# A vision tower's last chunk: its delta solve and output moved from a stage of their own into the end stage

## The chip, the cores and the metric

The kernel runs on one core of a Trainium2 chip. A core has a matrix engine (PE, with its weight loads, PEld, shown apart), a vector engine (DVE), a scalar engine (ACT), a general engine (POOL) and a sync engine (SP), which here only issues DMAs. Each engine takes its own instructions in order, and they wait for one another by semaphores. The time is the device time of one execution in microseconds (us); lower is better. Before the change it was 1849.73 us, the median of 3 runs (1849.12 to 1850.84).

## The reference, cut to what matters

64 images become sequences of 38 tokens (36 patches and 2 class tokens) of width 256. Two layers follow. The first is softmax attention and a mixture of experts. The second, which is where the change lies, is a delta-rule layer with a gated, normalised output, and a feed-forward network with ternary weights:

```python
def step(S, inp):                       # per head, over the 38 steps of an image
    qt, kt, vt, at, gkt = inp
    Sp = S * jnp.exp(gkt)[..., None]
    u = jnp.einsum('bhk,bhkv->bhv', at, Sp) + vt
    S = Sp + jnp.einsum('bhk,bhv->bhkv', kt, u)
    o = jnp.einsum('bhk,bhkv->bhv', qt, S)
    return (S, o)
...
gate = jax.nn.sigmoid(x @ Wg1 @ Wg2)
out = out * gate
mu = jnp.mean(out, axis=-1, keepdims=True)
var = jnp.mean(jnp.square(out - mu), axis=-1, keepdims=True)
out = (out - mu) * jax.lax.rsqrt(var + 1e-05) * norm_w
return out @ Wo
...
scale = jnp.maximum(jnp.mean(jnp.abs(w)), 1e-08)      # ternary weights of the FFN
w_t = jnp.clip(jnp.round(w / scale), -1.0, 1.0)
```

## The kernel before, in words

All activations stay in the core's memory: the residual `RES` by 19 tiles of 128 tokens, and the normalised input transposed, as a high and a low part (`XH`, `XL`), since products are made from split numbers. The program is a row of stages. A stage (`stage`) is a block in which every engine has its own list of instructions; at its end all engines meet at a barrier and the semaphores are cleared, so nothing of one stage runs beside another.

The delta rule is solved by chunks of 8 images, `CHUNKS` = 8. The recurrence of a chunk becomes a triangular system for u, and the work on it is a pipeline over the stages `delta_stage(..., c, nxt, z, y)`, called for k = 0 to 10: stage k projects chunk k (`nxt`), scores chunk k-1 (`c`), inverts the triangular blocks of chunk k-2 (`z`) and solves and outputs chunk k-3 (`y`). So the last stage, k = 10, has only `y` = 7.

The solve has 64 lanes (4 pairs of images by 16 heads), in two halves of 32, `j` (or `i`) = 0 and 1. For each half PE runs `first_half`, 64 small matmuls of the inverse with the values; ACT copies the result back (`first_back`, into `RX`); `remainder`, 64 matmuls, multiplies it with the off-diagonal block; DVE scales this and adds the values (`with_values`, two operations); `second_half`, 64 matmuls, uses the inverse again; ACT copies (`solution`); and `output`, 32 matmuls, gives the outputs of even and odd heads in PSUM banks. ACT and DVE then put the two together (`odd_out`, `whole_out`, into `OW`) and write high and low parts into `XH` and `XL` (`high_out`, `low_out`). One such fp32 matmul is two matmul instructions with two weight loads in the trace: the stage k = 10 has 448 in the program and 896 in the trace.

Then comes the end stage, `output_tail`. SP loads the FFN's weights (`ffn_w`, 1 MB twice, and the biases). PE makes for each tile t the gate (`gate`, one matmul) and the delta output in token rows (`token_rows`, four matmuls against the identity). ACT takes the sigmoid into `SG`, DVE multiplies it with the rows (`gated`, into `Y`) and takes statistics. The first 9 tiles (`LEAD`) and all 19 gates are done ahead of a loop. Still ahead of it DVE sums the weights' magnitudes (L1616), PE adds them over the partitions (L1481), DVE makes the scales (L1620 to L1624) and the inverse deviations of the first 9 tiles. The loop's turn j then normalises tile j (ACT L1502), transposes it (PE L1446, ACT L1507, DVE L1574), multiplies tile j-1 by the output weights (PE L1459), adds it to the residual with statistics (DVE), and normalises and transposes the sum of tile j-3 (L1517, L1470, L1522, L1600), with DVE's L1593 and L1595 for its scale and shift; it also makes the token rows and products of tile j+9. POOL meanwhile turns the weights to ternary, 16 slices of three operations (L1652 to L1657), as soon as the scales are there. The last stage, `ternary_ffn`, is the FFN.

Buffers are taken from one stack of memory. Those of the delta stages (`delta_buffers`) are given back before the FFN's weights get their place, in the same memory.

Of the kernel before, what the change touches and what calls it, by code (L numbers as in the profile page):

```python
# [18 lines left out]
F32 = mybir.dt.float32  # L19
# [295 lines left out]
def build_tower(nc, ins, out):  # L315
    with ExitStack() as whole:
        numbers = count()

        def sb(ctx, name, shape, dt=F32):
            name = f"{name}_{next(numbers)}"  # L320
            return ctx.enter_context(nc.sbuf_tensor(name, shape, dt))
# [964 lines left out]
def last_layer(nc, sb, psum, bank, ins, RES, BN, MV, STD, XN, XH, XL, xh_c, xl_c, ident, identb, hmask, out):  # L1286
# [9 lines left out]
    with ExitStack() as ctx:  # L1296
# [54 lines left out]

        with ExitStack() as inner:
            b = delta_buffers(sb, inner, XN)
# [11 lines left out]
        with ExitStack() as own:  # L1365
# [8 lines left out]
            Y = sb(own, "gated_out", [P, TILES, D])  # L1374
            SG = sb(own, "gate", [P, TILES, D])
# [3 lines left out]
                        w1, w2, b1, b2, up, down, ones, S, flat, tern, Y, SG, shift, eps)  # L1379
# [8 lines left out]
def output_tail(nc, bank, ins, RES, BN, MV, STD, XN, XH, XL, ident, identr, G1, wg2s, woh, wol,  # L1388
                w1, w2, b1, b2, up, down, ones, S, flat, tern, Y, SG, shift, eps):
# [4 lines left out]

    with stage(nc, "f_loaded", "eps_set", "ones_set", "abs_sum", "f_sum", "scale", "cut", "is_up", "is_down", "tern",
               "g_tile", "gate_ready", "o_tile", "y_ready", "bn_1", "mv_1", "std_1", "inv_1", "shift_1", "normed_1",
               "turned_1", "hi_1", "lo_1", "product", "summed", "bn_2", "mv_2", "std_2", "inv_2", "shift_2", "normed_2",
               "turned_2", "hi_2", "lo_2") as (
# [3 lines left out]
            turned_2, hi_2, lo_2):  # L1402
# [7 lines left out]
        def two_halves(tile):  # L1410
            return tile.rearrange("p (m t) -> p m t", m=HALVES)

# [7 lines left out]
        def _(pe):  # L1420
            def gate(t):
# [4 lines left out]
                nc.tensor.matmul(bank[2 + t % 2][:, 0:D], G1[:, cols(t)], wg2s[:, :],  # L1426
                                 start=True, stop=True).then_inc(g_ready, 1)

            def token_rows(t):
                if t >= TILES:  # L1430
                    return
                if t >= 2:
                    pe.wait_ge(y_ready, t - 1)
                for m in range(HALVES):
                    nc.tensor.matmul(bank[t % 2][:, m * P:(m + 1) * P], XH[:, m, cols(t)], identr[:, :],
                                     start=True, stop=False)
                    mm = nc.tensor.matmul(bank[t % 2][:, m * P:(m + 1) * P], XL[:, m, cols(t)], identr[:, :],
# [3 lines left out]
            def turn_gated(t):  # L1441
                pe.wait_ge(normed_1, t + 1)
                if t >= 2:
# [6 lines left out]
            def project(t):  # L1450
                pe.wait_ge(lo_1, t + 1)
                if t == 1:
                    pe.wait_ge(scaled, 1)
                if t >= 2:
# [8 lines left out]
            def turn_sum(t):  # L1463
                pe.wait_ge(normed_2, t + 1)
                if t < 2:
                    pe.wait_ge(gate_ready, TILES)
# [7 lines left out]
            for t in range(LEAD):  # L1474
                gate(2 * t)
                gate(2 * t + 1)
                token_rows(t)
            gate(2 * LEAD)
            pe.wait_ge(abs_sum, 2)
            pe.wait_ge(ones_set, 1)  # L1480
# [1057 lines left out]
```

## Time and profile before

| What | us |
|---|---|
| Median of 3 runs | 1849.73 (1849.12 to 1850.84) |
| The profiled execution's own time | 1850.91 |
| Its span in the trace | 1848.9 |
| PE busy | 1649.3 (89%) |
| DVE busy | 1103.9 (60%) |
| ACT busy | 689.7 (37%) |
| POOL busy | 332.6 (18%) |
| Stage k = 10, first to last instruction | 1664.68 to about 1690.5 |
| Gates and first token rows | 1691.17 to 1704 |
| Loop of the end stage | 1710.24 to 1767.8 |
| FFN | 1767.8 to 1848.9 |

Times within the trace are counted from the span's start. Busy PE counts overlapping matmuls, so it is not PE at its peak. "Idle before" in brackets is how long the engine stood before a row, and the name behind the arrow who released it; "issue" means that it waited for nothing that the profile shows, PEq for its own sequencer.

### The profile page before, as it was taken

How to read it: one execution, taken by the hardware profiler on the slowest of the kernel's cores; microseconds unless marked ns; L12 is line 12 of the kernel's file. 1: busy time of each engine (PE TensorE's matmuls, PEld its weight loads, DVE VectorE, ACT ScalarE, POOL GpSimd, SP SyncE). 2: the span in 40 equal slices, each digit the busy share in tenths (PEclk: the TensorE clock that was granted, in tenths of full speed). 3: DMA queues.
4: the chain of work that ended last, by engine and by line, in shares of the span. 5: the costliest groups of instructions: out<-in, count | busy, mean ns of one | idle time of the engine just before them, and what ended most of it. 6: DMA issues, size and time to landing. Idle time of an engine off the chain costs nothing. (4 is left out here: it accounts for less than half of the span.)

```text
span 1848.9 us, 49212 instructions
## 1 busy us (share of the span) xinstructions
PE 1649.3 (89%) x21601; PEld 1472.1 (80%) x21601; DVE 1103.9 (60%) x2417; ACT 689.7 (37%) x1436; POOL 332.6 (18%) x331
## 2 busy tenths in 40 slices
PE   8899968999999999999999999776889888766789
PEld 8787756998889999999999999455778776666668
DVE  7677757545554455555455565646655566553875
ACT  6466634222222222323232332253433334333642
POOL 5633344000000000000000000243222222200830
PEclk9999979999999999999999999777766766665889
DMA  6000011000010000001000000100000000001001
GB/s 210 1 3 2 2 49 46 1 24 23 1 46 1 24 23 24 24 1 46 1 24 24 1 1 1 38 2 2 3 3 4 3 3 3 4 4 51 1 12 44
DMA packets 11701, 36.10 MB, mean 20 GB/s; under 512 B 3400, under 2 KB 8032, under 8 KB 8928
## 3 DMA queue, kind: packets, MB, share of 16 engines
q1 hardware_dynamic: 11488, 32.97, 5.1%
q8 instruction: 170, 2.79, 0.6%
q14 instruction: 43, 0.35, 0.1%
HBM read 30.47 MB, written 2.49 MB: 18 GB/s over the span
## 5 line engine op out<-in xcount | busy, mean ns | idle before, releaser
L1126 ACT ACTIVATE hidden<-bank,moe_b 128x512 f32<-128x512 f32 (+1 forms) x320 | 213.4, 668 | 536.8 <-PE bank L1018 522.4
L1035 PE MATMUL bank<-moe_w2h,hidden_hi 128*128 128x256 f32 x1216 | 345.7, 284 | 0.0
L1035 PE MATMUL bank<-moe_w2l,hidden_hi 128*128 128x256 f32 x1216 | 344.0, 283 | 0.0
L1035 PE MATMUL bank<-moe_w2h,hidden_lo 128*128 128x256 f32 x1216 | 343.9, 283 | 0.0
L1160 DVE SCALAR_TENSOR_TENSOR residual<-bank,gates,residual 128x256 f32<-128x256 f32 x152 | 73.4, 483 | 290.4 <-PE bank L1035 290.4
L1018 PE MATMUL bank<-x_hi,moe_w1h 128*128 128x512 f32 (+1 forms) x640 | 243.7, 381 | 2.9 <-ACT hidden L1126 2.8
L1018 PE MATMUL bank<-x_lo,moe_w1h 128*128 128x512 f32 (+1 forms) x640 | 242.5, 379 | 0.0
L1018 PE MATMUL bank<-x_hi,moe_w1l 128*128 128x512 f32 (+1 forms) x640 | 242.0, 378 | 0.0
L1035 PEld LDWEIGHTS bank<-moe_w2h,hidden_hi 128*128 128x128 f32 x1216 | 233.1, 192 | 6.0 <-DVE residual L1160 4.3
L1035 PEld LDWEIGHTS bank<-moe_w2l,hidden_hi 128*128 128x128 f32 x1216 | 233.2, 192 | 1.2
L1035 PEld LDWEIGHTS bank<-moe_w2h,hidden_lo 128*128 128x128 f32 x1216 | 233.2, 192 | 0.0
L1148 DVE TENSOR_TENSOR hidden_lo<-hidden,hidden_hi 128x512 fp32r<-128x512 f32 (+1 forms) x320 | 215.2, 672 | 11.0
L1146 DVE CAST hidden_hi<-hidden 128x512 fp32r<-128x512 f32 (+1 forms) x320 | 133.1, 416 | 87.0 <-ACT hidden L1126 79.4
L1335 POOL MEMSET gate_low<- 80x2432 f32 x1 | 2.1, 2121 | 867.0 <-POOLq L70 867.0
L1018 PEld LDWEIGHTS bank<-x_hi,moe_w1h 128*128 128x128 f32 x640 | 120.3, 188 | 25.8 <-ACT hidden L1126 5.0
L1018 PEld LDWEIGHTS bank<-x_hi,moe_w1l 128*128 128x128 f32 x640 | 120.2, 188 | 20.4
L1018 PEld LDWEIGHTS bank<-x_lo,moe_w1h 128*128 128x128 f32 x640 | 120.3, 188 | 18.7
L2319 POOL TENSOR_TENSOR decay_steps<-log_f_parts,from_here 128x608 fp32r<-128x608 f32 x64 | 78.4, 1231 | 222.9 <-PE bank L1802 151.9
L2130 DVE TENSOR_TENSOR normed_tiles<-a_rows,inverse 128x2 f32<-128x2 f32 (+5 forms) x144 | 69.2, 480 | 3.3
L1825 PE MATMUL bank<-q_and_k,dk_in_pair 32*64 32x76 f32 x2048 | 35.7, 276 | 32.3 <-DVE out_whole L2214 22.6
L1825 PEld LDWEIGHTS bank<-q_and_k,dk_in_pair 32*64 32x64 f32 x2048 | 30.1, 159 | 40.1 <-issue 26.5
L2193 DVE TENSOR_TENSOR qk_and_ak<-bank,decay 128x304 f32<-128x304 f32 x128 | 51.6, 464 | 15.7 <-PE bank L1825 8.4
(315 smaller groups left out, 3268.8 us busy)
## 6 DMA issues: line engine op xcount, KB each, us to landing
moe_w<-in_moe_w SPq DMA_DIRECT2D x16, 1024.0 KB, 4.8
patches<-in_patches SPq DMA_DIRECT2D x7, 864.0 KB, 5.6
out<-residual SPq DMA_DIRECT2D x19, 128.0 KB, 1.7
ffn_w<-in_ffn_w SPq DMA_DIRECT2D x2, 1024.0 KB, 5.9
att_w<-in_att_w SPq DMA_DIRECT2D x1, 1536.0 KB, 9.2
delta_w<-in_delta_w SPq DMA_DIRECT2D x1, 1280.0 KB
patches<-in_patches SPq DMA_DIRECT2D x6, 144.0 KB, 3.0
tok_w<-in_tok_w SPq DMA_DIRECT2D x6, 128.0 KB, 2.6
```

Of the source, the lines that this page charges most:

```text
L1018: mm = nc.tensor.matmul(bank[i % 4][:, 0:n], left, right, start=(j == 0), stop=(j == len(passes) - 1))
L1035: mm = nc.tensor.matmul(bank[4 + n % 3][:, 0:D], left, right, start=(i == 0), stop=(i == len(passes) - 1))
L1126: nc.scalar.activation(H[:, i % 4, 0:n], bank[i % 4][:, 0:n], ACT.Relu, bias=b1[:, x, f:f + 1]).then_inc(acted, 1)
L1146: nc.vector.tensor_copy(HH[:, k % 2, f, 0:n], H[:, i % 4, 0:n]).then_inc(h_hi, 1)
L1148: nc.vector.tensor_tensor(HL[:, k % 2, f, 0:n], H[:, i % 4, 0:n], HH[:, k % 2, f, 0:n].bitcast(F32), ALU.subtract).then_inc(h_lo, 1)
L1160: nc.vector.scalar_tensor_tensor(out=RES[:, t, :], in0=bank[4 + n % 3][:, 0:D], scalar=G[:, t, x:x + 1], in1=RES[:, t, :], op0=ALU.mult, o ...
L1335: nc.gpsimd.memset(G1[:].bitcast(F32), 0.0).then_inc(done, 1)
L1825: mm = nc.tensor.matmul(psum[half(s), g, ts], KX[rows, m, 2 * p + s, e, :], QKc[rows, m, 2 * p + s].rearrange("p x t -> p (x t)"), start=T ...
L2130: nc.vector.tensor_tensor(PD[:, :, 0:t, 0:t], spread(AS[:, :, t, 0:t], 2, t), TT[:, :, 0:t, 0:t], ALU.mult).then_inc(t_mult, 1)
L2193: nc.vector.tensor_tensor(PA[:, c % 2, p, m * HPH:(m + 1) * HPH].rearrange("p (g e) x t -> p e g x t", e=2)[:, e], psum[:, 0:PPH, n * 2 * ...
L2319: nc.gpsimd.tensor_tensor(MS[:, b % 2], spread(LF[:, :, b // 2, heads].bitcast(F32), 3, SEQ), spread(spread(here[:, :], 1, HPH), 1, 2), AL ...
```

## The change

The call of `delta_stage` for k = 10 goes. Its work is written out in `output_tail`, among the gates and token rows. The buffers that it needs (`solve_buffers`) are taken from the other side of memory and live until the end stage is over; `PA` and `VH`, which were one buffer each for all chunks in flight, become lists of buffers. The gate is written into `Y` and multiplied there by the token rows; `SG` goes. Gates, rows and the loop use other PSUM banks, with waits to match. DVE's sums of magnitudes stand at two places, behind the seventh tile's statistics and right ahead of the loop; the scales, and PE's matmul for them, stand in the loop.

```diff
-            for k in range(CHUNKS + 3):
+            for k in range(CHUNKS + 2):
                 delta_stage(nc, psum, bank, b, k - 1 if 1 <= k <= CHUNKS else None, k if k < CHUNKS else None,
-                            k - 2 if 2 <= k < CHUNKS + 2 else None, k - 3 if k >= 3 else None)
+                            k - 2 if k >= 2 else None, k - 3 if k >= 3 else None)
...
-            Y = sb(own, "gated_out", [P, TILES, D])
-            SG = sb(own, "gate", [P, TILES, D])
+            Y = sb(own, "gate_then_gated", [P, TILES, D])
...
# PE, token_rows and project
+                if t == LEAD + 1:
+                    pe.wait_ge(o_whole, 4)
+                if t * P + P > y * CT:
+                    pe.wait_ge(o_lo, 4)
...
+            def remainder(i):
+                pe.wait_ge(u1_back, i + 1)
+                for lane in range(LANES)[lanes(i)]:
+                    for n in range(2):
+                        rows = slice(PAD * n, PAD * n + HB)
+                        mm = nc.tensor.matmul(bank[i][PAD * n + HB:PAD * n + HB + HALF, place(lane)],
+                                              pa_y[rows, lane, 1, HALF:SEQ], RX[rows, lane, :],
+                                              start=True, stop=True)
+                mm.then_inc(r_done, 1)
...
+            first_half(0)
+            gates_and_rows(0)
+            first_half(1)
+            gates_and_rows(1)
+            gates_and_rows(2)
+            remainder(0)
...
             gate(2 * LEAD)
-            pe.wait_ge(abs_sum, 2)
-            pe.wait_ge(ones_set, 1)
-            nc.tensor.matmul(bank[7][:, 0:2], ones[:, :], S[:, 0, :], start=True, stop=True).then_inc(total, 1)
+            output(0)
+            output(1)
             for j in range(TILES + 3):
                 if j < TILES:
                     turn_gated(j)
                 token_rows(j + LEAD)
                 if 0 <= j - 1 < TILES:
                     project(j - 1)
+                if j == 2:
+                    pe.wait_ge(abs_sum, 2)
+                    pe.wait_ge(ones_set, 1)
+                    pe.wait_ge(o_whole, 2)
+                    nc.tensor.matmul(bank[3][:, 0:2], ones[:, :], S[:, 0, :], start=True, stop=True).then_inc(total, 1)
...
# ACT
+            first_back(0)
+            gates(0, 1)
+            first_back(1)
+            gates(*range(2, 12))
+            solution(0)
+            gates(12, 13)
+            solution(1)
+            gates(*range(14, TILES))
             act.wait_ge(eps_set, 1)
             deviations(0)
+            odd_out(0, 0)
+            odd_out(0, 1)
             norm_gated(0)
+            odd_out(1, 0)
+            odd_out(1, 1)
             for j in range(TILES + 3):
+                if j == 1:
+                    for i in range(2):
+                        high_out(i, 0)
+                        high_out(i, 1)
...
# DVE
-                nc.vector.tensor_tensor(Y[:, t, :], bank[t % 2][:, 0:D], SG[:, t, :], ALU.mult).then_inc(y_ready, 1)
+                nc.vector.tensor_tensor(Y[:, t, :], row_bank(t)[:, 0:D], Y[:, t, :], ALU.mult).then_inc(y_ready, 1)
...
+            for t in range(3):
+                measured(t)
+            with_values(0)
+            measured(3)
+            with_values(1)
+            for t in range(4, 7):
+                measured(t)
+            magnitude(0)
+            measured(7)
+            measured(8)
             gated_stats(LEAD - 1)
...
             for j in range(TILES + 5):
                 if 0 <= j - 1 < TILES:
                     low_gated(j - 1)
+                if j == 2:
+                    for i in range(2):
+                        low_out(i, 0)
+                        low_out(i, 1)
+                if j == 3:
+                    scales()
...
+        "PA1": sb(ctx, "qk_and_ak1", [P, IP, HEADS, 2, SEQ], side="right"),
+        "VH1": sb(ctx, "values1", [P, IP, HEADS, HD], side="right"),
```

On PE, stage k = 10 and the start of the end stage stood like this before (`x128` are matmuls of the program; L1426 is a gate, L1435 and L1437 are token rows):

```order
L1882 MATMUL bank<-values,inverse_t 19x16 x128
L1894 MATMUL bank<-u_then_rest,qk_and_ak 19x16 x128
L1906 MATMUL bank<-u_then_rest,inverse_t 19x16 x128
L1922 MATMUL bank<-qk_and_ak 32x76 x64
L63 UNCONDITIONAL_BRANCH
L1419 UNCONDITIONAL_BRANCH
L1426 MATMUL bank<-delta_wg_parts,gate_low 128x256 x2
L1435 MATMUL bank<-ident_r,x_hi 128x128
L1437 MATMUL bank<-ident_r,x_lo 128x128
```

Now the end stage on PE begins so (L1522 is `first_half`, L1459 the gates, L1472 and L1474 the token rows):

```order
L1452 UNCONDITIONAL_BRANCH
L1522 MATMUL bank<-values_92,inverse_t 19x16 x64
L1459 MATMUL bank<-delta_wg_parts,gate_low 128x256 x2
L1472 MATMUL bank<-ident_r,x_hi 128x128
L1474 MATMUL bank<-ident_r,x_lo 128x128
L1472 MATMUL bank<-ident_r,x_hi 128x128
L1474 MATMUL bank<-ident_r,x_lo 128x128
L1522 MATMUL bank<-values_92,inverse_t 19x16 x64
L1459 MATMUL bank<-delta_wg_parts,gate_low 128x256 x2
```

The two halves of a step of the solve no longer stand in one piece of 128: six pieces of 64 have one or two groups of six gate and row matmuls between them, and the two outputs (64 together) follow the last gate.

On DVE, between the last statistics ahead of the loop and the loop's first product, stood before (L1616 the two magnitudes, L1567 and L1569 the inverse deviations, L1620 to L1624 the scales, L1550 the product):

```order
L1562 BN_AGGR mean_var<-bn 128x2 x2
L1616 TENSOR_REDUCE scales<-ffn_w_114 128x1
L1616 TENSOR_REDUCE scales<-ffn_w_115 128x1
L1567 RECIPROCAL std<-std 128x9
L1569 SCALAR_TENSOR_TENSOR minus_mean<-mean_var,std 128x9
L1620 TENSOR_SCALAR scales<-bank 128x2
L1623 TENSOR_SCALAR scales<-scales 128x2
L1624 TENSOR_SCALAR scales<-scales 128x2
L1550 TENSOR_TENSOR gated_out<-bank,gate 128x256
```

Now the same place reads (L1763 is `whole_out`, L1774 the second magnitude, L1691 the product):

```order
L1703 BN_AGGR mean_var<-bn 128x2 x2
L1708 RECIPROCAL std<-std 128x9
L1710 SCALAR_TENSOR_TENSOR minus_mean<-mean_var,std 128x9
L1763 SCALAR_TENSOR_TENSOR out_whole<-bank,in_pair,out_whole 128x152 x4
L1774 TENSOR_REDUCE scales<-ffn_w_118 128x1
L1691 TENSOR_TENSOR gate_then_gated<-bank,gate_then_gated 128x256
```

One magnitude has gone ahead, the four merges of the last chunk's output have come in, and the scales stand in the loop's turn 3.

## Rows read from the trace of the kernel before

**Rows 1.** The core by stretches: busy microseconds of each engine, granted clock, DMA share, GB/s

```profile
1664.68:1690.50 25.82, 16.48 (x896) 15.38 (x896) 4.99 (x12) 8.69 (x15) 0.00 (x0) 0.50 0.02 4
...
1691.17:1704.00 12.83, 12.39 (x55) 11.94 (x55) 6.94 (x25) 7.38 (x20) 0.00 (x0) 0.50 0.47 175
...
1710.24:1767.80 57.56, 39.65 (x230) 31.75 (x230) 47.61 (x169) 36.72 (x96) 40.67 (x48) 0.89 0.01 1
```

**Rows 2.** Timeline of PE in the solve-only stage: start, duration, line, matmuls merged, idle before

```profile
1664.71 2.81 PE L1882 MATMUL bank<-values,inverse_t 32*19 32x16 f32 x158 [1.39 <-PEq L70]
...
1675.46 1.74 PE L1894 MATMUL bank<-u_then_rest,qk_and_ak 32*19 32x16 f32 x93 [1.16 <-issue]
...
1678.93 2.32 PE L1906 MATMUL bank<-u_then_rest,inverse_t 32*19 32x16 f32 x128 [1.20 <-issue]
...
1682.67 1.84 PE L1906 MATMUL bank<-u_then_rest,inverse_t 32*19 32x16 f32 x98 [1.43 <-issue]
```

**Rows 3.** DMA from 1640 to 1720 us: rate in 2-us slices; queues: packets, MB, share

```profile
GB/s 8 0 8 0 8 0 8 0 8 0 0 0 8 0 8 0 8 0 8 0 8 8 0 8 0 0 254 414 400 56 0 0 0 0 0 0 0 0 4 0
...
q1 hardware_dynamic: 576, 2.23, 7.5%
...
q8 instruction: 13, 0.21, 1.1%
```

**Rows 4.** Timeline of PE in stage k = 7, solve and projections interleaved

```profile
1527.77 1.52 PE L1882 MATMUL bank<-values,inverse_t 32*19 32x16 f32 x109 [0.51 <-issue]
...
1531.52 2.11 PE L1894 MATMUL bank<-u_then_rest,qk_and_ak 32*19 32x16 f32 x115 [0.54 <-issue]
...
1535.38 2.32 PE L1894 MATMUL bank<-u_then_rest,qk_and_ak 32*19 32x16 f32 x128
...
1546.13 0.21 PE L1906 MATMUL bank<-u_then_rest,inverse_t 32*19 32x16 f32 x1 [0.89 <-issue]
```

**Rows 5.** Timeline of PE in the end stage, before the loop

```profile
1691.21 0.76 PE L1426 MATMUL bank<-delta_wg_parts,gate_low 80*128 80x256 f32 x2 [3.09 <-PEq L70]
...
1694.30 0.73 PE L1426 MATMUL bank<-delta_wg_parts,gate_low 80*128 80x256 f32 x2
...
1695.58 0.73 PE L1426 MATMUL bank<-delta_wg_parts,gate_low 80*128 80x256 f32 x2
...
1703.26 0.52 PE L1426 MATMUL bank<-delta_wg_parts,gate_low 80*128 80x256 f32 x1
```

**Rows 6.** Timeline of DVE, ACT and PE between the gates and the loop

```profile
1704.79 4.45 DVE L1616 TENSOR_REDUCE scales<-ffn_w 128x1 f32<-128x2048 f32 x2
...
1706.25 0.30 ACT L1496 ACTIVATE std<-mean_var,tail_eps 128x9 f32<-128x9 f32 x1
...
1709.59 0.60 ACT L1502 ACTIVATE normed_tiles<-gated_out,minus_mean,std 128x256 f32<-128x256 f32 x1 [3.04 <-DVE minus_mean L1569]
...
1711.71 0.42 DVE L1550 TENSOR_TENSOR gated_out<-bank,gate 128x256 f32<-128x256 f32 x1 [1.37 <-PE bank L1437]
...
1712.73 0.39 DVE L1574 TENSOR_TENSOR x_lo<-bank,x_hi 128x256 fp32r<-128x256 f32 x1
...
1713.18 0.58 PE L1459 MATMUL bank<-delta_wh,x_hi 128*128 128x256 f32 x1
```

**Rows 7.** Groups by line in the solve-only stage: busy, mean ns, idle before

```profile
L2214 DVE SCALAR_TENSOR_TENSOR out_whole<-bank,in_pair,out_whole 128x152 f32<-128x152 f32 x4 | 1.3, 370 | 9.5 <-ACT out_whole L2062 9.5
...
L2062 ACT ACTIVATE out_whole<-bank,in_pair 128x152 f32<-128x152 f32 x4 | 1.3, 379 | 2.0 <-PE bank L1922 2.0
```

**Rows 8.** Timeline of DVE and POOL, single rows of both stages

```profile
1689.47 0.98 DVE L2222 TENSOR_TENSOR x_lo<-out_whole,x_hi 128x152 fp32r<-128x152 f32 x4
...
1750.39 0.74 DVE L1595 SCALAR_TENSOR_TENSOR minus_mean<-mean_var,std 128x1 f32<-128x1 f32 x1
...
1760.49 0.16 DVE L1595 SCALAR_TENSOR_TENSOR minus_mean<-mean_var,std 128x1 f32<-128x1 f32 x1
...
1753.06 0.73 POOL L1657 TENSOR_TENSOR w_ternary<-is_up,is_down 128x256 fp32r<-128x256 f32 x1
```

More of the change, by code:

```diff
@@ L1472, in turn_sum, with place, first_half @@
                 turn.then_inc(turned_2, 1)
-            for t in range(LEAD):
+            def place(lane):
+                n = lane % (LANES // 2) * HD
+                return slice(n, n + HD)
+            def first_half(i):
+                for lane in range(LANES)[lanes(i)]:
+                    for n in range(2):
+                        rows = slice(PAD * n, PAD * n + HB)
+                        mm = nc.tensor.matmul(bank[i][PAD * n:PAD * n + HALF, place(lane)],
+                                              TS[rows, lane * HALF:(lane + 1) * HALF], vh_y[rows, lane, :],
+                                              start=True, stop=True)
+                mm.then_inc(u1_done, 1)
@@ new lines, in remainder @@
+            def remainder(i):
+                pe.wait_ge(u1_back, i + 1)
+                for lane in range(LANES)[lanes(i)]:
+                    for n in range(2):
+                        rows = slice(PAD * n, PAD * n + HB)
+                        mm = nc.tensor.matmul(bank[i][PAD * n + HB:PAD * n + HB + HALF, place(lane)],
+                                              pa_y[rows, lane, 1, HALF:SEQ], RX[rows, lane, :],
+                                              start=True, stop=True)
+                mm.then_inc(r_done, 1)
@@ new lines, in second_half @@
+            def second_half(i):
+                pe.wait_ge(rx_ready, i + 1)
+                for lane in range(LANES)[lanes(i)]:
+                    for n in range(2):
+                        rows = slice(PAD * n + HB, PAD * (n + 1))
+                        mm = nc.tensor.matmul(bank[i][PAD * n + HB:PAD * n + HB + HALF, place(lane)],
+                                              TS[rows, lane * HALF:(lane + 1) * HALF], RX[rows, lane, :],
+                                              start=True, stop=True)
+                mm.then_inc(u2_done, 1)
@@ new lines, in output @@
+            def output(i):
+                pe.wait_ge(u2_back, i + 1)
+                for p in (2 * i, 2 * i + 1):
+                    for m in range(HALVES):
+                        for n in range(2):
+                            for g in range(PPH):
+                                lane = p * HEADS + m * HPH + 2 * g
+                                mm = nc.tensor.matmul(
+                                    own_and_other(i, n)[32 * g:32 * g + 32, m, p % 2], UB[half(n), lane // 2, :],
+                                    pa_y[half(n), lane:lane + 2, 0, :], start=True, stop=True)
+                mm.then_inc(o_done, 1)
@@ L1604, in _, with measured @@
             nc.vector.memset(ones[:], 1.0).then_inc(ones_set, 1)
-            for t in range(LEAD):
+            def measured(t):
                 gated(t)
```

159 lines of the change are left out of this document (118 added, 41 removed), and 1 row of the table UB.

## Prediction, made before the changed kernel was run

> **What bounds the kernel now.** The chain of waits is of little use: it begins with the last stage, and that stage is not changed. So I went by stretches first. The last four delta-rule stages end in one (k = 10) that only solves and outputs chunk 7; it lasts 25.82 us, and PE is busy for 16.48 of it, DVE for 4.99, ACT for 8.69 [rows 1]. Then comes the end stage: gates and token rows for 12.8 us with PE busy 12.39, then a gap, then the loop over tiles. In the first two the granted clock is 0.50, the level of 1.2 GHz.
>
> Second, PE's timeline in the solve-only stage. 128 matmuls run at 18 ns each (2.32 us), then PE stands "issue" for 1.16 to 1.43 us; block starts are 3.47 and 3.74 us apart [rows 2]. There are six such stops, some 7 us in all. Each comes after 128 matmuls with 128 weight loads, 256 instructions. The DMA answer has an own queue for instructions: 13 packets, 0.21 MB, so 16 KB each, which is 64 bytes for each of 256 [rows 3]. I read the stops as PE waiting for its next block of instructions. In stage k = 7, where projections of some 1.7 us stand between the pieces of the solve, the stops shrink to 0.51, 0.54 and 0.89 us and the full block at 1535.38 has none [rows 4]. So big matmuls between small ones hide the supply. Gates and rows of one t are such work: 1.28 us for 6 matmuls (1694.30 to 1695.58) [rows 5], from 1691.21 to 1703.78, 12.57 us in all.
>
> The Trainium skill, "Runtime: NRT & Kernel Launch", section "Instruction fetch mechanics", also has blocks of 16 KiB, 256 instructions, fetched by a queue of the sequencer's own; but it says that the fetch is hidden because dispatch is slower than the fill. The first half agrees with rows 3, the second doesn't with rows 2. If it held here, the stops would have a cause that gates don't hide; that is the first rival below.
>
> Third, the gap. After the gates DVE sums the FFN weights' magnitudes, 4.45 us for both, and PE waits; the loop's first projection starts at 1713.18 [rows 6].
>
> **The change, part by part.** I measure from the first solve matmul, 1664.71 [rows 2], to the first projection, 1713.18 [rows 6]: 48.47 us before. The stage boundary goes, since the end stage now begins where k = 10 did.
>
> 1. PE's own work stays: 16.48 us of solve and output, 12.57 us of gates and rows, together 29.05, at the clock of rows 1.
> 2. Stops that are left. Lower end 0 (the gates between are 1.28 to 2.56 us, a stop at most 1.43); upper end 7, all stay. The nearest row is stage k = 7, whose stops add up to 1.94 us over six blocks [rows 4]. There every break is one piece of work; here two of them are double. I take 1.5.
> 3. The weights' loads move. SP issues them at the stage's start, so their 2.23 MB, which take four slices of 2 us [rows 3], now meet PE's instruction blocks; before, they ran under gates, which need 12 instructions in 1.28 us. An instruction packet takes 1.1% x 80 us x 16 / 13 = 1.1 us. Two blocks fall into the load. Shared engines might double a packet: 0 to 2.2 us. Nothing excludes more (last rival). I take 0.5, since there is slack behind the double gates.
> 4. Waits added between PE, ACT and DVE. u1 goes to ACT and back, the remainder to DVE (two operations) and back, u2 to ACT and back. In each place the order has at least one group of gates and rows (1.28 us) or the other half's block (2.3 us) between sender and receiver, and ACT and DVE are idle for half of the gates' stretch [rows 1]. Behind a waiting PE instruction stand only gates, for which ACT would wait too. 0 if covered; without cover six handovers of at most 0.7 us, 4. I take 0. DVE's magnitude of w1 (2.2 us) stands before the eighth tile's product, and PE waits there only for earlier tiles; it is hidden too.
> 5. From PE's last output to the first projection. The square root over nine tiles ended 3.3 us after the start of the last gate (1703.26 to 1706.55) [rows 5, 6]; the output blocks, now behind that gate, fill these 3 us, so both come together. Then, in ACT's and DVE's order: four odd_out at about 0.35 (each 379 ns, overlapping at the ends) [rows 7], 1.4; the first normalising 0.6 between them [rows 6]; the last whole_out 0.37 [rows 7]; the second magnitude, half of 4.45, 2.25; and product, statistics and low part of the loop's first turn, from 1711.71 to 1713.12, 1.4 [rows 6]. Sum 6.0. The first magnitude and the square root's table load are no longer exposed.
>
> 29.05 + 1.5 + 0.5 + 6.0 = 37.05, and 48.47 - 37.05 = 11.4 us earlier at the first projection.
>
> 6. In the loop. DVE gets four low_out, 0.98 us [rows 8], in turn 2; before it, DVE waits for PE there (1.37 us before the first product, and as much two turns later), so they are hidden; uncovered they cost 1.0. ACT's four high_out stand in turn 1 while DVE still sums magnitudes: 0. The three scale operations and their matmul go into turn 3, where DVE is the bound: 0.5.
> 7. POOL starts its 16 ternary slices only after these, so about 6 to 7 us later against the loop. Its two-input operation makes DVE's tiny shift operation take 0.74 instead of 0.16 us [rows 8]. Before, the first two or three slices ran while no such operation stood in DVE's row; now that many more meet it, each at up to 0.58, plus turns 2.7 instead of 2.1 us long at the end. 0 to 2; I take 1.1. POOL itself ended at 1753.79 [rows 8], 14 us ahead of the loop's end (1767.8) [rows 1]; 7 are left, so it does not become the bound.
> 8. Multiplying in place (Y over its own gate) and buffers at the other end of memory: same shapes, same counts; 0. That they lie there is what lets the loads start while the solve runs. The earlier delta stages run the same instructions: 0. The last stage, the FFN, has the same entry conditions.
>
> Gain 11.4 - 0.5 - 1.1 = 9.8 us. The profiled execution took 1850.91 us (span 1848.9), 1.2 above the median of 1849.73; I take the difference from the median: 1839.9, say 1840.
>
> **Rivals.**
> First: the stops are not hidden. For it: the skill's rule above, and that even in k = 7 some are left [rows 4]. Against: k = 7 has a third of them. Then 7 in place of 1.5: 1845.5.
>
> Second: more is won. The granted clock, 0.50 up to the loop before, may rise to 2.4 GHz within the merged stage, which keeps PE busy without a break for 30 us; the clock was 0.50 also in gates with 12.39 of 12.83 busy, which speaks against it [rows 1]. Then gates need half as long and the supply bounds: 2 x (896 + 55) instructions / 256 x 3.47 us = 25.8 in place of 31.05, and the time is 1834.7.
>
> Third, the other side: starvation. If an instruction packet does not share with the load but waits behind all of it, PE stands for the load's 7 us, then for a refill of 3.5, and, with the supply always behind from then on, the 5.5 us of the first rival come on top: 16 us, 1856. It is slower than before from a loss of 9.8 us on, measurably from 13.5. For it: no stretch of the trace has loads beside a fast instruction stream. Against: a packet of its own queue takes 1.1 us and one of the loads 7.5% x 80 x 16 / 576 = 0.17 us [rows 3], so taking turns costs little.
>
> **How the numbers follow.** Forecast 0.70, not hidden 0.15, more won 0.12, starvation 0.03. The likeliest gives 1840.0. The range, 1835.5 to 1845.3, leaves out the starvation and the far halves of the other two, and holds items 2, 3 and 7 at either end. A difference of 0.2%, 3.7 us, is what a measurement of this kernel can tell from none. Faster by more (under 1846.0): 0.94, which holds nearly all of the first three; within: 0.03; slower: 0.03.
>
> **What would show it.** The stage boundary before the end stage gone, and output(1) done about 31 us after the first solve matmul; "issue" stops of PE in the solve pieces adding up to 1 to 3 us, not 7; the first projection 37 us after the first solve matmul; the loop from there to its end about 1.5 us longer than 54.6 us (1713.18 to 1767.8), with POOL done some 7 us before that. I am wrong if the stops stay above 5 us, if stops of several microseconds stand in the first 10 us while the loads run, or if the loop grows by more than 3 us.

## The result, and the profile after

The changed kernel took 1839.33 us, the median of four runs (1837.96 to 1841.48), beside 1849.78 (1849.12 to 1850.84) for the kernel before: ratio 0.994, 95% interval 0.9925 to 0.9955, 10.4 us less. The forecast was 1840.0. A second set gave 1838.53 beside 1850.46, ratio 0.993 (0.9914 to 0.9945). The profiled execution has a span of 1839.7 us, 9.2 less than that of before.

The merged stage by stretches, as in [rows 1]: from the first solve matmul to the last output, from there to the first projection, and the loop to the FFN's first matmul. Behind the length of each stretch stand the busy times of PE, PEld, DVE, ACT and POOL, then granted clock, DMA share and GB/s.

```profile
1666.88:1697.20 30.32, 29.62 (x951) 27.95 (x951) 12.75 (x34) 10.69 (x25) 0.00 (x0) 0.51 0.21 77
1697.20:1703.44 6.24, 2.27 (x13) 1.95 (x13) 5.11 (x12) 4.74 (x15) 0.00 (x0) 0.73 0.01 3
1703.44:1759.50 56.06, 38.65 (x220) 30.88 (x221) 47.97 (x170) 35.11 (x93) 40.72 (x48) 0.83 0.00 1
```

The 951 matmuls of two stretches of before (896 and 55) stand in one of 30.3 us, with PE busy for 29.6 of it. PE's timeline there, beside [rows 2]: pieces of the solve (L1522, L1532, L1542), the last gate, the outputs (L1554), and the first projection (L1498).

```profile
1666.88 2.31 PE L1522 MATMUL bank<-values,inverse_t 32*19 32x16 f32 x128 [1.39 <-PEq L70]
...
1671.78 1.92 PE L1522 MATMUL bank<-values,inverse_t 32*19 32x16 f32 x104 [0.60 <-issue]
...
1680.14 2.47 PE L1532 MATMUL bank<-u_then_rest,qk_and_ak 32*19 32x16 f32 x128
...
1694.99 2.17 PE L1554 MATMUL bank<-qk_and_ak 64*32 64x76 f32 x128
...
1703.44 0.58 PE L1498 MATMUL bank<-delta_wh,x_hi 128*128 128x256 f32 x1 [1.64 <-DVE x_lo L1715]
```

One "issue" stop is left, of 0.60 us. The six of before add up to 6.9. Measured from the first solve matmul, the last output ends at +30.3 us and the first projection starts at +36.6; before it was +48.5.

The DMA of 1640 to 1720, beside [rows 3] (rate in 2-us slices, then the queues):

```profile
GB/s 0 8 0 8 0 8 0 8 0 8 0 0 0 29 295 401 364 44 8 0 8 0 8 0 8 0 8 0 8 0 0 0 0 0 4 0 0 0 0 8
...
q1 hardware_dynamic: 576, 2.23, 7.4%
q8 instruction: 14, 0.23, 1.2%
```

The load now lies at about 1668 to 1675, under the first pieces of the solve. From its first packet to the end of its last it takes 7.4 us, where it took 6.5 before. In the gap between outputs and loop, ACT and DVE now read like this, beside [rows 6]:

```profile
1696.22 1.28 ACT L1601 ACT_TABLE_LOAD   x1 [0.74 <-DVE mean_var L1703]
1697.52 0.30 ACT L1601 ACTIVATE std<-mean_var,tail_eps 128x9 f32<-128x9 f32 x1
1697.73 0.65 ACT L1645 ACTIVATE out_whole<-bank,in_pair 128x152 f32<-128x152 f32 x2
...
1699.21 0.66 DVE L1763 SCALAR_TENSOR_TENSOR out_whole<-bank,in_pair,out_whole 128x152 f32<-128x152 f32 x2 [0.38 <-ACT out_whole L1645]
1699.79 2.27 DVE L1774 TENSOR_REDUCE scales<-ffn_w 128x1 f32<-128x2048 f32 x1
1701.98 0.41 DVE L1691 TENSOR_TENSOR gate_then_gated<-bank,gate_then_gated 128x256 f32<-128x256 f32 x1
```

The root ends at 1697.8, 0.7 us after the last output, then come the merges, the second magnitude and the first turn's product. In the loop, beside [rows 8]: the last chunk's low parts (L1769), the first scale (L1779), the shift operation (L1736) in the middle and near the end, and POOL's first and last ternary operation.

```profile
1704.61 0.99 DVE L1769 TENSOR_TENSOR x_lo<-out_whole,x_hi 128x152 fp32r<-128x152 f32 x4
...
1708.15 0.15 DVE L1779 TENSOR_SCALAR scales<-bank 128x2 f32<-128x2 f32 x1
...
1740.30 0.74 DVE L1736 SCALAR_TENSOR_TENSOR minus_mean<-mean_var,std 128x1 f32<-128x1 f32 x1
...
1756.38 0.16 DVE L1736 SCALAR_TENSOR_TENSOR minus_mean<-mean_var,std 128x1 f32<-128x1 f32 x1
...
1708.68 0.97 POOL L1836 TENSOR_SCALAR is_up<-ffn_w,scales 128x256 f32<-128x256 f32 x1 [88.63 <-DVE scales L1783]
...
1751.06 0.73 POOL L1841 TENSOR_TENSOR w_ternary<-is_up,is_down 128x256 fp32r<-128x256 f32 x1
```

Where the 9.2 us of the two profiled executions are: -11.9 to the first projection, +1.4 in the loop (54.7 to 56.1), -0.9 in the FFN (81.0 to 80.2), and +2.2 in the stages ahead, where the change moves only buffers. Over the executions of this study the first solve matmul starts between 1657.1 and 1667.1 us, whatever the kernel, so a span is a poor measure here; stretches that begin at that matmul repeat better. The FFN comes in two lengths, 80.1 to 80.2 us and 81.0 to 81.1. The longer one stands in three traces (before, the run with more blocks, the last run), and these three alone show the granted clock at 0.50 for 3.4 us once more, from about 18 us after the FFN's first matmul. That stretch in the trace of before, and the same place after:

```profile
1786.00:1789.00 3.00, 3.00 (x8) 2.21 (x8) 2.90 (x7) 1.69 (x3) 0.00 (x0) 0.50 0.00 0
```

```profile
1777.70:1780.70 3.00, 2.61 (x14) 1.93 (x13) 2.90 (x7) 1.71 (x3) 0.00 (x0) 1.00 0.00 0
```

So the 0.9 us that the FFN is shorter in the trace of after is no gain of the change; the run with places alone, in the old order, has 80.1 too.

### The profile page after: what moved, and what is told of

Its sections match the earlier page's. It is cut to its first block and busy times, and to the rows that moved or that the text cites. A ratio compares the mean times of both kernels' runs of the same rounds, so it can differ in the third digit from the quotient of the medians.

```text
span 1839.7 us, 49193 instructions
## 1 busy us (share of the span) xinstructions
PE 1651.1 (90%) x21601; PEld 1473.6 (80%) x21601; DVE 1103.6 (60%) x2417; ACT 685.3 (37%) x1433; POOL 332.9 (18%) x331
```

## The experiments

My theory: PE cannot take small matmuls faster than one block of 256 instructions in some 3.5 us, and large matmuls between them hide that; what is lost again in the loop is DVE held up by POOL. The rivals: the gain comes from the boundary and the moved sums, not from the mixing; the stops have a cause of their own; the load slows the supply; the new places in memory do something. Each time is compared with the kernel before in its own set, since the sets differ: its median was 1850.46, 1849.62 and 1845.72 us in the three sets of the experiments. "To the projection" is always from the first solve matmul of the same execution.

**The changed kernel again**, in one set with the solve in one piece, the second magnitude among the gates and the first run of the scales ahead of the loop.

> The changed kernel once more, as the measure for the three kernels beside it. In its first trace the first projection came 36.6 us after the first solve matmul, with 0.6 us of "issue" stops on PE, and the loop from there to the FFN's first matmul took 56.1 us. Both theories expect the same again: about 1839.5 us, 0.6% under the kernel before.

Measured 1838.53 us; to the projection 36.0, loop 55.5, one stop of 0.61. The stretches up to the FFN repeat within 0.6 us.

**The solve in one piece.** The changed kernel with all six pieces of the solve ahead of all gates and rows; ACT and DVE follow.

```diff
-            first_half(0)
-            gates_and_rows(0)
-            first_half(1)
-            gates_and_rows(1)
-            gates_and_rows(2)
-            remainder(0)
...
+            for step in (first_half, remainder, second_half):
+                step(0)
+                step(1)
+            for t in range(LEAD):
+                gates_and_rows(t)
```

> The solve's six pieces stand in one block ahead of the gates, as they stood before, but in the merged stage; the outputs still follow the last gate. Theory (small matmuls run out of instructions, big ones between them hide the supply): the stops of 1.0 to 1.4 us come back after every 128 matmuls, five or six of them, 5 to 7 us; some of it before the gates, so the first projection comes 41 to 43 us after the first solve matmul and the kernel takes 5 to 6 us longer than the changed one, 1845. Rival (what was won is the stage boundary and the moved sums, the place among the gates is worth nothing): within 1 us of the changed kernel, 1839.5.

Measured 1847.96 us, ratio 0.9987 (0.9977 to 0.9996): 9.4 us slower than the changed kernel, where I had said 5 to 6. To the projection 45.0, so 9.0 of it are there. Without the mixing hardly anything is left of the gain; the boundary and the moved sums are worth 3.5 us in the trace (48.5 to 45.0) and 2.5 in the medians. PE's timeline of this run:

```profile
1667.00 2.81 PE L1522 MATMUL bank<-values,inverse_t 32*19 32x16 f32 x158 [1.39 <-PEq L70]
1671.62 1.75 PE L1522 MATMUL bank<-values,inverse_t 32*19 32x16 f32 x93 [1.81 <-issue]
...
1676.74 2.32 PE L1532 MATMUL bank<-u_then_rest,qk_and_ak 32*19 32x16 f32 x128 [2.84 <-issue]
1680.21 1.75 PE L1532 MATMUL bank<-u_then_rest,qk_and_ak 32*19 32x16 f32 x93 [1.16 <-issue]
...
1687.42 1.84 PE L1542 MATMUL bank<-u_then_rest,inverse_t 32*19 32x16 f32 x98 [1.43 <-issue]
```

The stops add up to 8.4, not 6.9; the two long ones lie beside or right behind the load, which runs to about 1675. A table load of ACT for the gates' sigmoid, 1.28 us at 1689.92, stands bare as well, since PE has only gates to go on with: 0.9 us of waiting. The square root's table load (1.28 us at 1704.79) begins only when the outputs end, because DVE's statistics are done later in this order, so that from the last output to the projection it takes 7.2 us, not 6.2. In sum: 7.8 more of stops, 0.9 for the sigmoid's table and 1.0 for the root's, less 0.7 by which PE's own work is shorter, 9.0.

**The same with the loads held back** until the last second-half matmul, to price the load alone.

```diff
+            sp.wait_ge(u2_done, 2)
             for dst, src in ((w1, "ffn_w1"), (w2, "ffn_w2"), (b1, "ffn_b1"), (b2, "ffn_b2")):
```

> The block version (solve in one piece, then gates), with the weights' loads held back until the last second-half matmul is done. If the load beside the solve is what stretched two stops to 1.81 and 2.84 us, the six stops go back to those of the kernel before, 0.95 to 1.43 us each, sum 6 to 7 us in place of 8.4, and the first output ends about 36 us after the first solve matmul, not 37.8. The rival, that these two stops have to do with the place in the program (more instructions of ACT and DVE in one stage): the sum stays at 8 or more. The loads, 7 us, then end some 7 us after the solve, under the gates; DVE's magnitude waits for them but still ends before the gates do, so the first projection is at +43 to +43.5 and the time 1846 to 1847 us; should the magnitude be late, the projection is at +45 and the time as that of the block version, 1848.

Measured 1841.84 beside 1845.72 us, ratio 0.9977 (0.9967 to 0.9986). That is under the 1846 to 1847 that I had said, as the kernel before is lower in this set too. To the projection 42.8.

```profile
1664.83 1.74 PE L1523 MATMUL bank<-values,inverse_t 32*19 32x16 f32 x93 [0.73 <-issue]
...
1668.85 2.31 PE L1533 MATMUL bank<-u_then_rest,qk_and_ak 32*19 32x16 f32 x128 [1.75 <-issue]
1672.59 1.74 PE L1533 MATMUL bank<-u_then_rest,qk_and_ak 32*19 32x16 f32 x93 [1.43 <-issue]
...
1679.53 1.84 PE L1543 MATMUL bank<-u_then_rest,inverse_t 32*19 32x16 f32 x98 [1.15 <-issue]
```

The stops add up to 6.3, and the last output ends 2.2 us earlier. In the medians' distances to before it is 1.4, and their intervals overlap. One stop of 1.75 stands there with no load at all, and the sum of the stops varies too, as the run with places alone will show, so two traces prove little by it. The packets of the instruction queue tell more. In the first 10 us from the first solve matmul there are three of them here (1661.3 to 1671.3) and two in the solve in one piece (1667 to 1677), beside the load:

```profile
q8 instruction: 3, 0.05, 1.8%
```

```profile
q8 instruction: 2, 0.03, 1.2%
```

By their shares each takes some 0.96 us in both (1.8% x 10 x 16 / 3 and 1.2% x 10 x 16 / 2), so beside the load a packet takes no longer. What comes later is its start: in the trace's packet records the second one begins 7.3 us after the first solve matmul with the load and 5.2 without (4.9 in the three traces of kernels with the old stage). So the load holds the supply up by 2.1 us here, which agrees with the 2.2.

**More blocks in the kernel before.** Stage k = 10 gets 128 more of the program's small matmuls, into two banks that nobody reads: 512 instructions, two blocks, that neither DVE nor ACT waits for.

```diff
+            for again in range(2 if z is None and y is not None else 0):
+                for lane in range(LANES)[lanes(0)]:
+                    for s in range(2):
+                        rows = block_rows(2 * s)
+                        nc.tensor.matmul(psum[PAD * s:PAD * s + HALF, 4 + again, place(lane)],
+                                         TS[rows, lane * HALF:(lane + 1) * HALF], vh_y[rows, lane, :],
...
```

> The kernel before, with the first step of the solve in its last delta stage done twice: 128 more matmuls of the program, 256 with their 256 weight loads in the trace, into two banks that nothing reads, with no wait added. Theory (blocks of 256 instructions come every 3.5 to 3.7 us): the stage grows by two blocks, 7.0 to 7.5 us. Rival (the stops come from hand-overs or from anything bound to the steps of the solve): it grows by the matmuls' own time, 2 x 2.3 = 4.6 us.

Measured 1855.04 beside 1849.62 us, ratio 1.0032 (1.002 to 1.0044). In the trace the last output ends 7.5 us later, for 4.6 us of matmuls (256 in the trace, at 18 ns):

```profile
1664.79 0.66 PE L1940 MATMUL bank<-values,inverse_t 32*19 32x16 f32 x29
1666.59 2.31 PE L1940 MATMUL bank<-values,inverse_t 32*19 32x16 f32 x128 [1.15 <-issue]
1670.61 1.74 PE L1940 MATMUL bank<-values,inverse_t 32*19 32x16 f32 x93 [1.71 <-issue]
...
q8 instruction: 6, 0.10, 2.0%
```

The last row is of 1659 to 1680: six packets of 16 KB. So each block costs 3.7 us (7.5 / 2), where PE needs 2.3 for it. The supply is the bound; the medians, 5.4 us, say less than the trace, and their interval (3.7 to 8.1) holds it. That the stops are the supply can also be read from the packet records of the kernel before: ahead of each of its six stops one packet started 1.1 to 1.2 us after PE's block of matmuls had begun, it took 0.9 to 1.3 us, and PE went on 1.3 to 1.5 us after its end. Of the five blocks between the stops one took 3.74 us and its packet 1.27; the others took 3.47 and their packets 0.92 to 0.96.

**Twice the load** in the changed kernel: w1 is fetched twice more, into buffers that POOL overwrites later.

```diff
+            for t in (up, down):
+                sp.dma_start(t[:].rearrange("p (k f) -> p k f", k=HALVES), ins["ffn_w1"]).then_inc(again, 16)
```

> The changed kernel with 1 MB twice more loaded behind the weights, into buffers that are free until POOL starts; so the load lasts about 14 us instead of 7 and meets four blocks of instructions instead of two. Theory (an instruction packet takes turns with the load's packets): stops of PE in the solve grow by under 1 us, the time by under 1 us. Rival (starvation, the packet waits for the load): a stop of 5 us or more while the load runs, and 5 to 10 us more in all.

Measured 1841.78 beside 1849.62 us, ratio 0.9947 (0.9931 to 0.9964). That is 7.8 us under the kernel before, where the changed kernel is 10.4 to 11.9 under it. To the projection 39.0, 3.0 more than in the changed kernel's second run. PE's timeline:

```profile
1663.29 1.92 PE L1525 MATMUL bank<-values,inverse_t 32*19 32x16 f32 x104 [0.59 <-issue]
...
1669.77 2.11 PE L1535 MATMUL bank<-u_then_rest,qk_and_ak 32*19 32x16 f32 x116 [1.50 <-issue]
...
1673.79 1.38 PE L1535 MATMUL bank<-u_then_rest,qk_and_ak 32*19 32x16 f32 x72 [0.19 <-issue]
```

I had expected under 1 us. A load of 2.23 MB is covered by gates and their slack; one of 4.33 MB is not: the supply comes late, one stop of 1.5 appears, and small ones follow. Starvation, where a block waits for the whole load, is not seen either: with 12.9 us of load no stop is longer than 1.5.

**Only the places in memory.** The kernel before with the solve's buffers at the other end of memory, as lists, and the gate multiplied in place; the order of the work stays.

```diff
-            Y = sb(own, "gated_out", [P, TILES, D])
-            SG = sb(own, "gate", [P, TILES, D])
+            Y = SG = sb(own, "gate_then_gated", [P, TILES, D])
...
+        "PA1": sb(ctx, "qk_and_ak1", [P, IP, HEADS, 2, SEQ], side="right"),
+        "VH1": sb(ctx, "values1", [P, IP, HEADS, HD], side="right"),
```

> The kernel before, with the change's memory part alone: the solve's buffers at the other end of memory, the buffers of chunks in flight as lists, and the gate multiplied in place. Theory: no difference, within 1 us of 1849.8; each delta stage as long as before. Rival (where buffers lie, or writing over an operand, costs or gains): more than 2 us either way.

Measured 1850.33 beside 1849.62 us, ratio 1.0007 (0.9996 to 1.0017). No effect, as expected. To the projection 50.1 here, with stops of 8.6 in all and no load beside them: the sum itself varies by some 1.6 us (6.9 in the trace of before) from one execution to another.

**The second magnitude among the gates** too, behind the sixth tile's statistics.

```diff
+            measured(4)
+            measured(5)
             magnitude(0)
+            measured(6)
+            magnitude(1)
...
-            magnitude(1)
```

> The second magnitude moves from right ahead of the loop to behind the seventh tile's product, the first one goes one tile earlier, into the gap of 3.1 us that DVE has there in the trace of the changed kernel. Theory (the second magnitude, 2.27 us, stands alone on the way from PE's last output to the first projection): the first projection comes 1.9 to 2.2 us earlier, about 34.5 us after the first solve matmul, and the kernel takes 2 us less, 1837.5. Rival (PE with the tenth tile's rows, or ACT, is as late): under 0.7 us.

Measured 1836.62 us, ratio 0.9922 (0.9907 to 0.9936), 1.9 less than the changed kernel in the same set, though the two intervals overlap. From the last output to the projection 4.6 us, not 6.2. In this trace the projection is still at +35.9, for the outputs end 1.5 us later than in the changed kernel's second run: the stops add up to 1.0, 0.4 more, and PE is busy for 1.1 us more. The next five instruction packets after the second took 1.25 to 1.45 us here and 0.96 to 1.23 there; why is open. The two runs of the next experiment have the same order up to the outputs, end them at +29.9 and reach the projection at +34.5, so the later outputs belong to this execution and the 1.6 us to the change.

**The scales ahead of the loop as well**, with PE's matmul for them behind the outputs, so that POOL starts earlier.

```diff
-                if j == 3:
-                    scales()
...
+            inverses(0)
+            scales()
             for i in range(2):
                 whole_out(i, 0)
```

> As the kernel before this one in the list (both magnitudes early), and PE's matmul for the scales and the three scale operations stand ahead of the loop, where PE and DVE wait for ACT. POOL starts 9 us earlier against the loop. Theory (POOL's two-input operations hold up DVE's shift operation in the last turns, and the scales cost 0.5 us in turn 3): another 1 to 2 us less, about 1836, with the last turns of the loop 2.1 to 2.4 us long instead of 2.7. Rival (the loop's length is set elsewhere): the same time as the kernel with early magnitudes alone, 0.3 us either way.

> The version with both magnitudes among the gates and the scales ahead of the loop, a second time, on the chip of the two others, so that the one-input version is compared with it directly: 1835 us (1833.5 to 1836.5), loop 54.4 us, shift operation 0.5 to 0.74 us in about nine turns. If its first result was a lucky chip, it is at 1837 or more.

Measured 1834.91 beside 1850.46 us, ratio 0.9908 (0.9893 to 0.9923), and in a later set 1831.96 beside 1845.72, ratio 0.9927 (0.9914 to 0.9939). The loop is 54.4 and 54.2 us, 1.1 and 1.3 shorter than in the changed kernel's second run. The second time it was 1.5 us below my range, in a set in which the kernel before is 4.7 lower; against that kernel it gained less than the first time (13.8 us, not 15.6).

**POOL with one-input operations.** The last of the three ternary operations takes one input in place of two, so the lower mask is left out of the weights: it shows the time only.

```diff
-                    nc.gpsimd.tensor_tensor(tern[i][:, qs], up[:, qs], down[:, qs], ALU.subtract).then_inc(ternary, 1)
+                    nc.gpsimd.tensor_scalar(tern[i][:, qs], up[:, qs], 1.0, None, ALU.mult).then_inc(ternary, 1)
```

> The changed kernel, where POOL's third operation of each ternary slice reads one operand instead of two (it copies the upper mask and leaves the lower one out, so the FFN's weights are not the reference's). Theory (POOL's two-input operation holds up DVE's shift operation): that operation stays at 0.16 to 0.3 us in all 19 turns, where 7 of them took 0.5 to 0.74 in the changed kernel's trace; the turns from the twelfth on shrink from 2.7 towards 2.3 us and the loop by 2 to 4 us. POOL's own time should change little. Rival (the turn's length comes from ACT and DVE, the hold-up is beside it): the loop stays within 0.7 us.

Measured 1833.21 beside 1849.62 us, ratio 0.9909 (0.9895 to 0.9922). The loop is 53.1 us, 2.4 less than in the changed kernel's second run and 3.0 less than in its first. Groups of the shift operation on DVE and the third ternary operation on POOL, first of the changed kernel, then of this one:

```profile
L1736 DVE SCALAR_TENSOR_TENSOR minus_mean<-mean_var,std 128x1 f32<-128x1 f32 x19 | 7.1, 373 | 0.6
...
L1841 POOL TENSOR_TENSOR w_ternary<-is_up,is_down 128x256 fp32r<-128x256 f32 x16 | 11.7, 732 | 2.4 <-POOL is_down L1837 0.3
```

```profile
L1736 DVE SCALAR_TENSOR_TENSOR minus_mean<-mean_var,std 128x1 f32<-128x1 f32 x19 | 4.4, 233 | 0.6
...
L1841 POOL TENSOR_SCALAR w_ternary<-is_up 128x256 fp32r<-128x256 f32 x16 | 13.7, 854 | 2.6 <-POOL is_down L1837 2.6
```

The one-input operation is itself slower (854 for 732 ns), and still the loop is shorter: the two-input one held DVE up. The shift operation's longest instance is 0.39 us here, where I had said 0.3. The medians say more than the loop, 16.4 us under the kernel before in place of 10.4 to 11.9; where the rest of that comes from no trace shows. That the clock does it is unlikely: it was 0.89 in this loop, and 0.88 in the two of 54.4 and 54.2 us above.

**All of it, with the full computation.** The version above with early magnitudes and scales, and on POOL three operations of one input each: weight times the inverse scale, at most 1.25; at least -1.25, plus 12582912, which rounds to a whole number; minus 12582912.

```diff
-                    nc.gpsimd.tensor_scalar(up[:, qs], flat[i][:, qs], S[:, 2, i:i + 1], None, ALU.is_gt).then_inc(ups, 1)
...
-                    nc.gpsimd.tensor_tensor(tern[i][:, qs], up[:, qs], down[:, qs], ALU.subtract).then_inc(ternary, 1)
+                    nc.gpsimd.tensor_scalar(up[:, qs], flat[i][:, qs], S[:, 2, i:i + 1], 1.25,
+                                            ALU.mult, ALU.min).then_inc(ups, 1)
+                    pool.wait_ge(ups, n + 1)
+                    nc.gpsimd.tensor_scalar(down[:, qs], up[:, qs], -1.25, 12582912.0,
+                                            ALU.max, ALU.add).then_inc(downs, 1)
+                    pool.wait_ge(downs, n + 1)
+                    nc.gpsimd.tensor_scalar(tern[i][:, qs], down[:, qs], 12582912.0, None,
+                                            ALU.subtract).then_inc(ternary, 1)
```

> The version with both magnitudes among the gates and the scales ahead of the loop (1834.91 us before), and POOL's three operations per slice replaced by three with one input each: weight times inverse scale, at most 1.25; at least -1.25, plus 12582912, which rounds; minus 12582912. The hold-up theory: the loop's first product to last is 2 to 3 us shorter than the 54.4 us of that version, about 51.5 to 52.5, the shift operation stays at 0.16 us in all turns; time 1832 us (1830.5 to 1833). Rival, POOL becomes late since its three operations now follow one another: the loop stays at 54 us or longer, time 1835 or more. Second rival, the two gains overlap (what the earlier scales win is the same hold-up): no less than the 1833.2 us of the run with one-input operations alone.

Measured 1828.74 beside 1845.72 us, ratio 0.9908 (0.9894 to 0.9921), 3.2 us less than the two-input version in the same set, and 1.8 below my range, which came from another set. It beats both kernels, the changed one by some 5 to 6.5 us, if each is taken by its distance to before (17.0, and 10.4 to 11.9). Its loop, its shift operation, and POOL's last operation:

```profile
1692.00:1744.20 52.20, 34.91 (x220) 27.12 (x219) 44.45 (x167) 34.71 (x94) 46.74 (x47) 0.93 0.00 1
...
L1737 DVE SCALAR_TENSOR_TENSOR minus_mean<-mean_var,std 128x1 f32<-128x1 f32 x19 | 4.1, 217 | 0.6
...
1741.77 0.86 POOL L1842 TENSOR_SCALAR w_ternary<-is_down 128x256 fp32r<-128x256 f32 x1
```

The loop is 52.2 us, 2.0 less than with two inputs; the FFN is the longer of its two lengths in this execution (81.1), which hides 1.0 of it in the span. The rival on overlap is not settled by ratios (0.9908 here, 0.9909 for the run with one-input operations alone), but the traces speak against it: to the projection plus loop is 87.1 us here and 89.3 there. Little more is to be had in this way: POOL is busy for 46.7 us and ends 1.6 us before the FFN begins. The shift operation did not stay at 0.16 in all turns, as I had said, but at 0.16 to 0.41.

## Why the prediction was right, step by step

**Reading of the bound.** Right. The six stops were instruction supply: they come and go with the number of blocks and with what stands between them, and in the kernel before each ends 1.3 to 1.5 us behind a packet of the instruction queue. By the Trainium skill, "Runtime: NRT & Kernel Launch", section "Instruction fetch mechanics", they should not exist, since the fetch is hidden behind dispatch. The runs disagree, with 3.7 us for each added block.

**Items 1 and 2**, work and stops left: 29.05 + 1.5 + 0.5 forecast to the end of the last output, 31.05; measured 30.3. The stops came out at 0.60, not 2.0; PE's busy time at 29.6, for single pieces of the solve take up to 2.58 us now, not 2.32. I took the nearest row, stage k = 7, at a third of the old stops; here nearly all are hidden. I had also not looked at the clock of that stage: it was 0.99 from 1523 to 1530 and 0.50 from 1534 on, so the first of its three stops fell under another clock than this solve's. The stops were 1.4 us too high and PE's work 0.6 too low; that the two offset each other in part is luck.

**Item 3**, the load: 0.5, and it is inside those 0.60. The size is right and the reason is not: I had reckoned with longer packets, and beside the load none is longer, but they start later, by 2.1 us at the second one in a bare solve. The outputs end 2.2 us later there, and 3.1 later with twice the load in the mixed stage. The gates' slack pays for it, not the small size of the packets.

**Item 4**, added waits: 0. No row of PE among the solve's pieces has a wait for ACT or DVE behind it.

**Item 5**, from the last output to the projection: 6.0 forecast, 6.2 to 6.3 measured. The root's table load is not fully covered, against what I had said; it ends 0.3 us after the outputs, which is the difference.

Sum: first projection at 37.05 forecast, 36.6 and 36.0 measured in the two traces.

**Items 6 and 7**, the loop: 0.5 and 1.1, together +1.6 forecast; +1.4 and +0.8 measured in the two traces (56.1 and 55.5 after 54.7). The low parts cost nothing but the wait they fill: DVE waits 0.69 us behind them. The shift operation takes 7.1 us in 19 instances, 0.8 more than before, and DVE's turns (from one shift operation to the next) stay at 2.5 to 3.0 us up to 1754, 50.6 us after the first projection, where before they fell to 2.3 and then 2.1 us from 1756 on, 42.8 us after it. POOL ends at 1751.8, 7.7 us before the loop does (about 7 forecast). That POOL is the cause was argued then; the one-input run shows it. The clock is not the main cause of the longer loop, though it was 0.83 in this one and 0.91 in that of before: at 0.87 the loop took 55.9 us in the order of after (the solve in one piece) and 54.9 in that of before (the run with more blocks), and at 0.80 (the second magnitude among the gates) it took no more than 56.0.

**Item 8**: 0, and the run with places alone shows it, within its interval (0.7 us less to 3.1 more). The 0.9 us of the FFN is the clock of one execution, as said above.

The whole gain was 9.8 forecast, and 10.4 and 11.9 measured by the medians; that the forecast lies within 0.7 us of the first set is closer than its terms were.

**Rivals.** "Not hidden" (1845.5) is out by the stops. "More won through the clock" (1834.7) as well: the granted clock was 0.51 over the merged solve, the level of 1.2 GHz. Starvation did not come with twice the load either. Where I would have been wrong is the worth of the parts: I held the mixing to be worth 5.5 us and the rest 4.3, and by the medians it is 9.4 and 2.5. The mixing hides the old stops, 5.7 of the 6.3 that stand there without a load, which is what I had said; but it also hides the 2.2 us that the earlier load brings and 1.9 us of two table loads, which show only when it is taken away. These I had not counted.

## What to carry to other kernels

Small matmuls that PE finishes faster than their instructions arrive (here 128 of them, 256 instructions, in 2.3 us where a block needs 3.5 to 3.7, in one trace up to 4.0) gain from large ones between them, and large transfers belong beside the large ones. Where the order of a merged stage is written, the worth of a part is found by taking it out of the new kernel, not by counting what it removed from the old one. An engine off the critical path can still stretch the one on it: look for one and the same tiny operation with two durations (0.16 and 0.74 us here) and for what runs beside the long ones.

## What was not expected of the hardware

- DVE's shift operation, 128x1 with two inputs, took 0.74 us beside POOL's two-input operation and at most 0.41 beside one-input ones (mean 217 to 233 ns, for 333 and 373 in the two kernels). The Trainium skill, "SBUF — State Buffer", section "SBUF: two separate sides", has a DVE operation with two inputs from this memory and a POOL operation that reads it share a pair of ports, which whichever starts first holds for its whole instruction. With POOL's two-input operation this agrees (the shift starts 0.02 us behind one of 0.73 us, takes 0.73 and ends with it); with the one-input ones, 0.85 to 1.15 us long, it does not: in the changed kernel the shift took 0.16 us at 1722.57 inside one of POOL's at 1722.18 that took 0.93, and 0.41 beside one of 1.15 in the last run.
- Beside 2.23 MB of loads the instruction supply of a bare solve lost 2.2 us, though its packets have a queue of their own and took no longer (0.93 and 0.97 us for the first two). They started late, the first at +2.4 instead of +1.2 us from the first solve matmul, the second at +7.3 instead of +5.2. What holds the start back is open.
- The FFN of the same instructions takes 80.1 or 81.0 us. The longer ones have one more stretch of 3.4 us at the lower clock, 18 us into it (three of thirteen traces), with the kernel before and the last one among them.
